# Attention of a macaron block: outputs kept turned, one inverse of the sums per batch, output product in pieces

## What is computed

```python
qkv = hidden_states @ Wqkv
scores = einsum('bqhd,bkd->bhqk', q, k) * scale + alibi        # causal
probs = softmax(scores, axis=-1)
attn = einsum('bhqk,bkd->bqhd', probs, v).reshape(B, S, H)
x = x + attn @ Wo
```

## Time and profile before

| | us |
|---|---|
| median of three runs (461.68 to 462.88) | 462.54 |
| the profiled execution: time, span | 463.63, 461.9 |
| PE busy in the span | 411.6 (89%) |
| DVE, ACT, POOL busy | 260.0, 180.6, 163.5 |
| attention's main loop to the second feed-forward's first matmul | 198.63 to 334.83 |

### The profile page before, as it was taken

One profiled execution on the slowest core, in us unless ns is written; L12 is line 12 of the kernel. 1 busy time (PEld: TensorE's weight loads), 2 busy tenths in 40 slices (PEclk: granted clock), 3 DMA queues, 4 the chain that ended last, 5 costly groups with the idle time before them and its releaser, 6 DMA issues.

```text
span 461.9 us, 8466 instructions
## 1 busy us (share of the span) xinstructions
PE 411.6 (89%) x2848; PEld 289.2 (63%) x2849; DVE 260.0 (56%) x729; ACT 180.6 (39%) x300; POOL 163.5 (35%) x230
## 2 busy tenths in 40 slices
PE   0899869999969979979999899798999889999973
PEld 0687568888646757646564565343587568888651
DVE  5489503333367945888883984633249933322457
ACT  1321235656111222166662472573532316656300
POOL 2701315665303853333431242342001053666300
PEclk9999998999998989999999999999999979999997
DMA  7999973533397479212220200010120042544278
GB/s 220 309 374 312 330 238 119 180 114 136 115 322 249 134 186 188 73 40 78 72 78 3 72 4 6 2 72 23 48 92 1 1 136 71 180 126 138 102 278 312
DMA packets 48620, 63.88 MB, mean 138 GB/s; under 512 B 7750, under 2 KB 28070, under 8 KB 48548
## 3 DMA queue, kind: packets, MB, share of 16 engines
q1 hardware_dynamic: 40220, 41.51, 28.6%
q0 software_dynamic: 6368, 19.19, 12.9%
q10 hardware_dynamic: 2000, 2.76, 2.1%
HBM read 46.06 MB, written 19.79 MB: 143 GB/s over the span
## 4 chain that ended last, share of the span: by engine, by line
PE 59%; DVE 17%; SPq 8%; DMA 8%; issue 4%; POOL 2%; ACT 1%; ACTq 0%; POOLq 0%; DVEq 0%
PE ps L1453 14%; PE ps L1460 7%; PE ps L1607 6%; SPq L320 5%; PE ps L1579 5%; PE ps L1522 4%; PE ps L1438 3%; DMA w<-in_L_ffn_ew_dram 3%; PE ps L1551 3%; PE ps L1317 3%; DVE arena L1161 2%; PE ps L1553 2%; PE ps L1565 2%; PE ps L1589 2%; SPq L343 2%
## 5 line engine op out<-in xcount | busy, mean ns | idle before, releaser
L1161 DVE TENSOR_REDUCE arena<-ps 128x3 f32<-128x384 f32 x128 | 67.3, 551 | 16.9 <-PE ps L1553 15.9
L1453 PE MATMUL ps<-arena,wj 128*128 128x128 f32 x608 | 76.5, 280 | 0.0
L1453 PEld LDWEIGHTS ps<-arena,wj 128*128 128x128 f32 x608 | 73.6, 197 | 1.0 <-issue 1.0
L764 ACT ACTIVATE arena<-ps 128x768 f32<-128x768 f32 x64 | 51.9, 812 | 48.8 <-PE ps L1567 48.0
L594 POOL TENSOR_SCALAR_AFFINE_SELECT arena<-arena 128x512 f32<-128x512 f32 x64 | 40.9, 640 | 81.5 <-ACT arena L764 81.2
L1058 DVE SCALAR_TENSOR_TENSOR arena<-ps,arena 128x128 f32<-128x128 f32 x38 | 13.3, 351 | 88.6 <-ACT arena L680 88.6
L1317 PE MATMUL ps<-arena,turns 128*128 128x256 f32 x256 | 57.5, 380 | 0.0
L1317 PEld LDWEIGHTS ps<-arena,turns 128*128 128x128 f32 x256 | 48.1, 190 | 8.2 <-issue 2.1
L526 POOL DMA_INDIRECT y_dram<-arena x38 | 38.5, 1012 | 41.4 <-DVE arena L1065 31.9
L521 POOL DMA_INDIRECT arena<-xn_dram,arena x34 | 33.3, 980 | 50.5 <-DVE arena L998 25.2
L1460 PE MATMUL ps<-w,arena 128*128 x76 | 39.6, 602 | 4.2 <-DVE arena L1058 4.2
(11 more groups left out here) (190 smaller groups left out, 609.7 us busy)
## 6 DMA issues: line engine op xcount, KB each, us to landing
arena<-y_dram SPq DMA_DIRECT2D x16, 512.0 KB, 8.0
arena<-q_dram SPq DMA_DIRECT2D x36, 128.0 KB, 2.6
xn_dram<-arena SPq DMA_DIRECT2D x16, 256.0 KB, 6.2
w<-in_L_ffn_ew_dram SPq DMA_DIRECT2D x4, 1024.0 KB, 11.5
q_dram<-arena SPq DMA_DIRECT2D x16, 192.0 KB, 2.4
x<-_attn_hidden_states_dram SPq DMA_DIRECT2D x4, 512.0 KB, 6.1
out_dram<-x SPq DMA_DIRECT2D x8, 256.0 KB, 5.5
turns<-in_L_ffn_sw_dram ACTq DMA_DIRECT2D x3, 512.0 KB, 7.4
```

Source lines behind the costliest of these rows:

```text
L764: act.activation(pr[:, n % 2, pair, :], ps[:, bank:bank + 2, :].rearrange("p a b -> p (a b)")[:, 0:768], ACT.Exp).then_inc(sem("exp"), 1)
L1161: dve.tensor_reduce(m3[:, h:h + 1, :], ps[:, bank, 0:3 * P].rearrange("p (n k) -> p n k", n=3), AX_X, ALU.max).then_inc(sem("s_max"), 1)
L1453: ins = pe.matmul(o, wj[:, par, c, n * INTER:(n + 1) * INTER], xgT[:, par, c, :], start=(c == 0), stop=(c == KC - 1))
```

## The change

The outputs are never turned. `vv` now alternates values and ones, and an even step takes its values into the even rows and the sums into the odd rows, an odd step the other way round. ACT copies even steps straight into `aT`, the operand of the output product, and odd steps into `odd`; the SP queue copies the values of `odd` into `aT`, and one row of sums per head pair into `sums`. When a batch is complete, `invert` (in q = 2 of the next batch) takes one reciprocal of 128x256 and splits it in three bf16 parts; `inverse_rows` (PE, q = 3 and 4) repeats each to its 16 rows by a matmul with 0/1 columns; DVE multiplies 128x512 at a time; `out_part` is a quarter of an output product, two in each of four places in q = 5, 6, 7. In batch 3 it is done otherwise: each pair's sums are copied to all rows by DMA and `normalise_last` works on one pair. `wo` is loaded with its rows in the new order by two DMAs, and the constant `cb` grows from 512 to 1024 bf16 columns.

```diff
-B_UP, B_ONE, B_ID, B_MASK, B_END = 0, 128, 256, 384, 512
+B_UP, B_ONE, B_ID, B_MASK, B_SEL, B_END = 0, 128, 256, 384, 512, 1024
...
+    for c in range(4):
+        const_b[:, B_SEL + c * P:B_SEL + (c + 1) * P] = i[:, None] == (i // 32 * 32 + 2 * c + i % 2)[None, :]
...
             for b in range(BATCH):
+                sums_of_even(4 * b)
+                odd_in(4 * b)
+                sums_of_even(4 * b + 1)
                 if b + 2 < BATCH:
                     q_rows(b + 2, 0, HEADS // 2)
+                odd_in(4 * b + 1)
                 if b + 1 < BATCH:
                     m_rows(b + 1, 0)
+                sums_of_even(4 * b + 2)
+                odd_in(4 * b + 2)
+                sums_of_even(4 * b + 3)
                 if b + 2 < BATCH:
                     q_rows(b + 2, HEADS // 2, HEADS)
+                odd_in(4 * b + 3)
...
+            def odd_in(p):
+                b, c = p // KC, p % KC
+                last = b + 1 == BATCH
+                sp.wait_ge(sem("oT"), 2 * p + 2)
+                into, rows = (sums[(c + 1) % 2], slice(0, P, 2)) if last else (sums[b % 2], slice(2 * c, P, 32) if c else slice(0, P, 2))
+                sp.dma_start(into[rows.start + 1::rows.step], odd[rows]).then_inc(sem(f"odd_in{p % 2}"), 16)
+                sp.wait_ge(sem(f"even_sums{p % 2}"), 16 * (p // 2 + 1))
+                sp.dma_start(aT[b % 2][1::2, c], odd[1::2]).then_inc(sem(f"odd_in{p % 2}"), 16)
...
+                else:
+                    if p >= 1:
+                        act.wait_ge(sem(f"odd_in{(p - 1) % 2}"), 32 * ((p - 1) // 2 + 1))
+                    act.copy(odd[:], ps[:, PS_O, 0:SEQ]).then_inc(sem("oT"), 1)
...
+            def invert(b):
+                for par in range(2):
+                    dve.wait_ge(sem(f"even_sums{par}"), 32 * (b + 1))
+                    dve.wait_ge(sem(f"odd_in{par}"), 64 * (b + 1))
+                link(dve.reciprocal(sums[b % 2], sums[b % 2]))
+                link(dve.tensor_copy(inverse[:, 0], sums[b % 2]))
+                link(dve.tensor_tensor(rest_of, sums[b % 2], inverse[:, 0], ALU.subtract))
+                link(dve.tensor_copy(inverse[:, 1], rest_of))
+                dve.tensor_tensor(inverse[:, 2], rest_of, inverse[:, 1], ALU.subtract).then_inc(sem("inverse"), 1)
+            def normalise(b, half):
+                dve.wait_ge(sem("inverted"), 2 * b + half + 1)
+                two = aT[b % 2][:, 2 * half:2 * half + 2].rearrange("p c t -> p (c t)")
+                dve.tensor_tensor(two, ps[:, PS_A, :], two, ALU.mult).then_inc(sem("normed"), 1)
+            def normalise_last(c):
...
+                dve.reciprocal(s, s).then_inc(sem("a_rec"), 1)
+                dve.wait_ge(sem("a_rec"), c + 1)
+                dve.tensor_tensor(aT[b % 2][:, c, :], aT[b % 2][:, c, :], s, ALU.mult).then_inc(sem("normed"), 1)
...
+            def inverse_rows(b, half):
+                pe.wait_ge(sem("inverse"), b + 1)
...
+                for c in (2 * half, 2 * half + 1):
+                    for k in range(3):
+                        ins = pe.matmul(ps[:, PS_A, c % 2 * SEQ:(c % 2 + 1) * SEQ], cb[:, B_SEL + c * P:B_SEL + (c + 1) * P], inverse[:, k],
+                                        start=(k == 0), stop=(k == 2))
...
+            def out_part(b, t, c):
+                pe.wait_ge(sem("normed"), 2 * b + c // 2 + 1 if b + 1 < BATCH else 2 * b + c + 1)
+                ins = pe.matmul(ps[:, at_bank(b, t), :], aT[b % 2][:, c, t * P:(t + 1) * P], wo[:, c, :], start=(c == 0), stop=(c == KC - 1))
...
-                        turn_back(n - 2)
+                    if q in (3, 4) and b >= 1:
+                        inverse_rows(b - 1, q - 3)
+                    if q == 5 and b >= 1 and more:
+                        pe.wait_ge(sem("m_parts"), 2 * b + 3)
+                        out_part(b - 1, 0, 0)
+                        out_part(b - 1, 0, 1)
```

More of the change, by code:

```diff
@@ L366, in ffn_sp @@
                 nc.sync.wait_ge(sem("s_z"), NT)
-                nc.sync.dma_start(wo, wo_in.rearrange("(c p) n -> p c n", p=P)).then_inc(sem("wo_in"), 16)
+                for g in range(2):
+                    nc.sync.dma_start(wo[g::2], wo_in.rearrange("(c g p) n -> g p c n", g=2, p=P // 2)[g]).then_inc(sem("wo_in"), 16)
         def att_sp():
@@ L786, in att_act @@
                 xnT_copy(1, t)
-            for t in range(QT):
-                turned(BATCH - 1, t)
             xnT_copy(1, 4)
@@ L1265, in att_dve @@
                         maxima(b + 1, 4 * q + 1, PS_S + 1)
-                    if n >= 2:
-                        normalise(n - 2)
+                    if q == 2 and b >= 1:
+                        invert(b - 1)
+                    if q == 4 and not more:
+                        normalise(b - 1, 1)
+                    if q in (5, 7) and not more:
+                        normalise_last(q // 2 - 2)
+                    if q == 6 and b >= 1:
+                        residual(b - 1, 0)
+                    if q == 0 and b >= 2:
+                        residual(b - 2, 1)
                     if more:
@@ L1691, in att_pe @@
                         max_turn(b + 1, 0)
-                    if b >= 1 and q in (5, 6):
-                        pe.wait_ge(sem("normed"), n - 1)
-                        out_product(b - 1, q - 5)
+                    if b >= 1 and more:
+                        if q == 5:
+                            out_part(b - 1, 0, 2)
+                            out_part(b - 1, 0, 3)
+                        if q == 6:
+                            pe.wait_ge(sem("att_x"), QT * (b - 1) + 1)
+                        if q >= 6:
+                            out_part(b - 1, 1, 2 * q - 12)
+                            out_part(b - 1, 1, 2 * q - 11)
@@ L1695, in att_pe @@
+                    if not more:
+                        if q == 5:
+                            pe.wait_ge(sem("s_max"), HEADS * BATCH)
+                        if q in (5, 6):
+                            for c in range(KC):
+                                out_part(b - 1, q - 5, c)
+                        if q == 7:
+                            pe.wait_ge(sem("m_parts"), 2 * b + 2)
+                            out_part(b, 0, 0)
             last = 8 * BATCH - 1
-            turn_back(last - 1)
+            pe.wait_ge(sem("att_x"), QT * (BATCH - 1))
@@ L1697, in att_pe @@
             xn_turn(1, 0)
             weigh(last)
-            xn_turn(1, 1)
-            turn_back(last)
-            xn_turn(1, 2)
-            xn_turn(1, 3)
-            attn_turn(BATCH - 1, 0)
-            pe.wait_ge(sem("oT"), last + 1)
-            attn_turn(BATCH - 1, 1)
+            for t in range(1, 4):
+                xn_turn(1, t)
+            pe.wait_ge(sem("oT"), last + 1)
+            out_part(BATCH - 1, 0, 1)
+            for c in range(KC - 2):
+                out_part(BATCH - 1, 1, c)
@@ L1706, in att_pe @@
+            for t in range(QT):
+                out_part(BATCH - 1, t, KC - 2)
             xn_turn(1, 4)
-            out_product(BATCH - 1, 0)
             xn_turn(1, 5)
-            out_product(BATCH - 1, 1)
+            for t in range(QT):
+                out_part(BATCH - 1, t, KC - 1)
             pe.wait_ge(sem("exp"), 2 * 8 * BATCH)
```

154 lines of the change are left out of this document (71 added, 83 removed).

## The result

The changed kernel took **464.61 us** (median of 20 runs, 462.52 to 466.64), the kernel before 462.32 us in runs beside it (458.48 to 465.97): a ratio of 1.0048, 95% interval 1.0028 to 1.0067. The forecast was 464.8. The profiled execution of the changed kernel took 462.52 us (span 460.8), the quickest of its 20, so the windows are compared first, and the totals after that.

The account below looks back on a forecast made before the run. Bound: score, maximum, score in batches 0 to 2, ACT in batch 3. Terms -0.25 + 2.9 + 1.9 - 5.9 + 0.1 + 3.6 = +2.3 on 463.6, 1.1 above the median: 464.8 us; range 457.5 to 468.0, forecast's own 462.5 to 467.

Parts of the forecast that it names:

- The reciprocal: In `invert`, DVE's reciprocal on 256 columns takes 1.8 us, making `invert` 3.6 us.
- rival 1: Fast reciprocal in `invert`, 0.46 us: 4.1 us saved, smaller idle stretches save another 2.4, about 458.3 us; chance 0.22.
- Plain steps: Steps of the q loop stay at 2.88 us, bound by score, maximum, score; removing `turn_back` gains nothing in batches 0 to 2.
- Batch 0: First batch's window: gains 0.25 us from the removed small reciprocal and product of `normalise`, to 24.4 us.
- Batch 1: Second batch's window: steps sum to 36.7 us, +2.9, with PE idle 3.0 us behind `invert`; clock fall extra.
- Batch 2: Third batch's window: steps sum to 37.35 us, +1.9, with q=2 at 6.31 us; clock fall extra.
- Batch 3: Last batch's window: waits tying PE to DVE go, 42.23 us becomes 36.3, -5.9; PE waits 2.9 us in `inverse_rows`.
- The clock: After the three new idle stretches of PE the granted clock falls to half, costing 1.2 us each, +3.6.
- The constant: At the start, the 128 KB larger constant and second issue for wo cost 0.1 us.
- Clock holds: Rival: the clock does not fall after most new idle stretches; 461 to 463 us, no change; chance 0.15.
- Late rows: Rival: odd-row copies land late, 0.5 to 1 us in each of four pairs, `invert` starts later; 467 to 468 us; chance 0.13.
- Everything gained: Rival: all work PE no longer does is gained, 2.2 us of turning in batches 1 and 2; 455 us; no chance given.

Follow-up runs that it names:

- d_turns: The changed kernel with two unread fp32 transposes put back ahead of the third score in four plain steps of batch 0; 460.60 us, one run.
- b_fill: The changed kernel with unread matmuls filling PE's idle stretches in batches 1 to 3; 460.99 us, 0.9968 of the kernel before.
- p_const: Constant loaded in two parts, on the changed kernel with GpSimd splitting, reordered copies and later repeated inverses; 456.86 us, 0.9884 of the kernel before.
- four alike profiles: Profiles of the change, its unaltered repeat (464.56 us), d_turns and g_order; 2, 2, 2 and 3 falls in the loop.
- g_order: The changed kernel with the last odd rows' copies issued ahead of the second half of `q_rows`; 463.93 us, 0.9989 of the kernel before.

## Why the prediction was right, and where it was not

**The total** came within 0.2 us of the forecast, and the sign and mechanism were right: long work of DVE ahead of one maximum, an idle stretch of PE, a fall behind it. Its terms were less good than its sum, and that they met so closely is luck.

**The reciprocal**: 1.8 forecast from the 44 ns, 1.75 measured, 6.8 ns a column; with it rival 1 fell. (By the Trainium skill, VectorE: DVE Perf Modes, Walkthrough, read as 8 cycles an element, the estimate was 2.1 us, which the trace puts 0.35 too high.) `invert` from 233.27 to 236.6 is 3.3 us for my 3.6: the casts took 0.29 where no POOL operation held them, for 0.36.

**Plain steps** stay 2.88 (d_turns). Batch 0 is 24.48 for a forecast of 24.4.

**Batch 1**: idle 3.12 for 3.0, with the late rows in it, which I had put two steps ahead of `invert`: that was wrong (0.55 us in the profile). Without its fall the batch is 36.4 us (37.99 less 1.6) for my 36.7.

**Batch 2**: 37.35 forecast, 35.9 measured (37.50 less 1.6). This step failed. For q = 2 I had 6.3 us: PE's own part 2.9 and, since the first maximum comes late, a stretch of 3.4. Its own part was 3.25 (from one weighing to the next) and the stretch 2.40. The rest lies mostly in q = 4 and q = 5, 9.0 us for my 9.6; they were as much too long in batch 1, where other steps made up for half of it.

**Batch 3**: 36.3 forecast, 35.55 measured, without a fall; its stretch of 2.77 was forecast as 2.9. That the ties to DVE were what the change removed there was argued from the rows and not tried: no run put the turns back in batch 3.

Without the falls of the changed kernel the loop thus went from 136.20 us (198.63 to 334.83) to 132.3, **3.9 us less, where my terms gave 1.35 less**. The 136.20 hold the one fall of the kernel before, in batch 3, as my 42.23 did; how much of the gain there is that fall and how much the waits around it, no run shows.

**The clock**: three falls at 1.2, 3.6 us, was forecast; 2.25 falls at 1.6 us, 3.6 us, was found, the same product from two errors. b_fill shows that falls cost time: with none left in the loop, the change is 0.3% faster than before. The runs of the change (32) had a mean granted clock of 0.9705, those of before (60) 0.9756, and means of 464.34 and 462.94 us. A line through each set puts both kernels at the same time where the clock is 0.97: 464.46 and 464.37 us. That the two kernels differ by their clock fits this, but it is a comparison of averages over whole executions: the lines fall by some 230 and 250 us per unit of clock, while one fall of 3.4 us lowers the mean clock of 461 us by 0.0037 and costs 1.6 us in the loop, 430 us per unit, so the mean clock counts falls that cost less, or other things with them. It does not show that the clock alone separates the kernels: in the loop the change has 1.25 falls more than the kernel before, some 2 us by this price, an estimate.

**The constant**: 0.1 us forecast for 128 KB more at the start. The first matmul is 0.2 to 0.7 us late (p_const undoes most of it, in one profile), and the first weighing stands at 205.1 us on average in twelve profiles of changed kernels (202.6 to 206.6) for 204.0 in both profiles of before. p_const, with the small first load, has it at 205.37. The number of falls ahead of the loop does not explain the 1.1 us: it is three in both profiles of before and 2.75 on average in the twelve, and the five of them with three start the first weighing at 205.6 on average. Where the 1.1 us come from stays open.

So the loop brings 3.9 less 3.6, 0.3 us less than the profiled execution of before, and the start some 1.1 more: +0.8 on 463.63, 464.4, beside the mean of 464.34. What follows the loop I left out; it differs from one execution to the next by its falls. My sum was +2.3: too high by 2.5 in the loop, too low by 1.0 at the start. Then I took 1.1 us off, as far as the profiled execution stood above the median, and that brought the forecast within 0.4 us of what the parts give. So errors of 2.5 us in the loop, 1.5 of them in batch 2, 1.0 at the start and the 1.1 of the profiled execution cancelled.

**Rivals.** Clock holds (461 to 463): it held in 3 of the 12 stretches of the four alike profiles, not in most. Late rows: real, 0.6 us in batch 1 (g_order) and 0.4 in batch 3, not the 0.5 to 1 us in each of four pairs that I priced. Everything gained: excluded by d_turns in the plain steps of batch 0.
